# Norm of two attention heads: 16 normalising operations written on GpSimd instead of VectorE

## The chip, the core and the metric

The kernel runs on one core of a Trainium2 chip. Its time is the device time of one execution in microseconds (us); the time of a kernel is the median of several executions. The engines of the core are TensorE (PE in the profile, its weight loads PEld), VectorE (DVE), ScalarE (ACT), GpSimd (POOL) and SyncE (SP), which issues the transfers. Each engine works through its own list of instructions in the order in which they are written, and stops at an instruction until the semaphores that it names have reached their counts.

## The reference

Four layers, each an attention step and a feed-forward step, on x of 8 batches x 128 tokens x 128 features, float32. What the change touches is the layer norm ahead of the attention of layers 1 and 3 (the kernel's first and third softmax attention; layer 0's is another kind):

```python
def _layernorm(x, axis=-1, eps=1e-05):
    m = jnp.mean(x, axis=axis, keepdims=True)
    v = jnp.var(x, axis=axis, keepdims=True)
    return (x - m) / jnp.sqrt(v + eps)
...
    x = x + jnp.tanh(g_ffn[0]) * _L0_ffn_ref(_layernorm(x, axis=-1), ...
    x = x + jnp.tanh(g_xattn[1]) * _L1_xattn_ref(_layernorm(x, axis=-1), ctx_1024, ctx_1024, ...
    x = x + jnp.tanh(g_ffn[1]) * _L1_ffn_ref(_layernorm(x, axis=-1), ...
    x = x + jnp.tanh(g_xattn[2]) * _L2_xattn_ref(_layernorm(x, axis=-1), ctx_1024, ctx_1024, ...
    x = x + jnp.tanh(g_ffn[2]) * _L2_ffn_ref(_layernorm(x, axis=-1), ...
    x = x + jnp.tanh(g_xattn[3]) * _L3_xattn_ref(_layernorm(x, axis=-1), ctx_1024, ...
    x = x + jnp.tanh(g_ffn[3]) * _L3_ffn_ref(_layernorm(x, axis=-1), ...
```

Queries of an attention come from the normed x, keys and values from the context, which does not change. So keys and values can be projected while x is still being finished; queries cannot.

## The kernel before

Every tensor lies with the 128 tokens of a batch on the partitions; X and XN are 128 x 8 batches x 128. Work on all tokens is done in two halves of four batches. There is no scheduler: the functions below write each engine's list by hand, and an engine meets its work in that order.

A norm numbered k runs in these steps. VectorE writes the statistics of a half (`half_stats_dve`: four `bn_stats` into STAT, L394, and four `bn_aggr` into MV, L400). GpSimd makes 1/sqrt(v + eps) of a half in two instructions on 128x4 numbers (`norm_pool`: VE, L447, then the power RSTD, L449). Then each batch is normed, one instruction of 128x128 per batch (`ln_apply`, L410, into XN; each raises the semaphore `ln_xn` by one). TensorE transposes XN batch by batch into PSUM (`turn_pe`, L460), ScalarE copies the half to fp16 as XH (`turn_act`, L466), and VectorE writes the remainder XL (`turn_dve`, L472).

The head of attention a (`head_pe`, `head_act`, `head_dve`) runs 16 projections of keys and queries, numbered e = 0 to 15 (e 0 to 3 keys of the first half, 4 to 7 keys of the second, 8 to 11 and 12 to 15 queries), and two of values. One projection of keys or queries is three matmuls of 512 columns (L228), one ScalarE copy (`proj_act`, L1781, semaphore `p_hi`) and one VectorE operation of 128x512 (`proj_dve`, L1788, semaphore `p_lo`). TensorE may run at most four projections ahead of VectorE, by waits on `p_lo`. Projections 13 to 15 are woven into the first rows of the attention, whose maxima VectorE takes with L1914.

Heads a = 0 and a = 2 use norms k = 2 and k = 6. TensorE's order there: projections 2, 3, the values, the four transposes of the first half, projections 4 and 5, the four transposes of the second half, projections 6 to 12. The middle attention, a = 1, has a head of its own, which is not touched. `att_pool`, the GpSimd part of the attention, follows `norm_pool(pool, 2)` and `norm_pool(pool, 6)` in GpSimd's list. It already norms six of eight batches of the next norm itself, with the same `ln_apply`, in attention 0 and in attention 2.

Of the kernel before, what the change touches and what calls it, by code (L numbers as in the profile page):

```python
# [40 lines left out]
def gated_mix_program(nc, t, out):  # L41
# [5 lines left out]
    with ctx:  # L47
# [5 lines left out]
        def sem(name):  # L53
            if name not in sems:
                sems[name] = ctx.enter_context(nc.semaphore(name))
            return sems[name]
# [351 lines left out]
        def ln_apply(eng, k, b, s, to, src=X):  # L408
            eng.wait_ge(sem("ln_rstd"), NB * k + b + 1)
            eng.tensor_scalar(XN[:, to, :], src[:, b, :], MV[:, s, 0:1], RSTD[:, s:s + 1],  # L410
                              ALU.subtract, ALU.mult).then_inc(sem("ln_xn"), 1)
# [18 lines left out]
        def half_stats_dve(dve, k, i):  # L430

            for b in range(4 * i, 4 * i + 4):
                if k == 4:
                    dve.wait_ge(sem("x_quant"), b + 1)
                ln_stats(dve, k, b, b)
            for b in range(4 * i, 4 * i + 4):
                ln_mean(dve, k, b, b)

        def half_apply_dve(dve, k, i):
            for b in range(4 * i, 4 * i + 4):  # L440
                ln_apply(dve, k, b, b, b)

        def norm_pool(pool, k, halves=(0, 1)):
            for i in halves:
                h = slice(4 * i, 4 * i + 4)
                pool.wait_ge(sem("ln_mv"), NB * k + 4 * i + 4)
                pool.tensor_scalar(VE[:, h], MV[:, h, 1], 1e-5, None, ALU.add).then_inc(sem("ln_var"), 4)  # L447
                pool.wait_ge(sem("ln_var"), NB * k + 4 * i + 4)
                pool.tensor_tensor(RSTD[:, h], VE[:, h], EPS[:], ALU.pow).then_inc(sem("ln_rstd"), 4)  # L449


        def turn_pe(pe, j, k, halves=(0, 1), at=(0, 1)):
            if j == 0:
                pe.wait_ge(sem("ld_eye"), 16)
            for b in range(4 * halves[0], 4 * halves[-1] + 4):
                if j == 1 and b >= 4:
                    fill_pe(pe, 4, 2 if b == NB - 1 else 4)
                pe.wait_ge(sem("ln_xn"), NB * k + b + 1)
                to = tail_bank(7, 8) if j == 1 and b == 7 else bank(at[b // 4])[:, 128 * (b % 4):128 * (b % 4) + 128]
                pe.transpose(to, XN[:, b, :], EYE[:])\  # L460
                    .then_inc(sem("xt_turned"), 1)
# [7 lines left out]
        def turn_dve(dve, j, halves=(0, 1), at=(0, 1)):  # L469
            for i in halves:  # L470
                dve.wait_ge(sem("xt_high"), NB * j + 4 * (i + 1))
                dve.tensor_tensor(XL[:, 4 * i:4 * i + 4, :].rearrange("p b s -> p (b s)"), bank(at[i]),  # L472
                                  XH[:, 4 * i:4 * i + 4, :].rearrange("p b s -> p (b s)"),
                                  ALU.subtract).then_inc(sem("xt_low"), 4)
# [1217 lines left out]
        def moe_x_dve(dve, m, i):  # L1692

            g = 4 + (0, 2, 3)[m]
            dve.wait_ge(sem("y_turned"), 2 * m + i + 1)
            xs = X[:, 4 * i:4 * i + 4, :].rearrange("p b d -> p (b d)")
            dve.scalar_tensor_tensor(xs, bank(i), G[:, g:g + 1], xs, ALU.mult, ALU.add).then_inc(sem("x_moe"), 1)
            if m < 2:
                dve.wait_ge(sem("x_moe"), 2 * m + i + 1)
# [84 lines left out]
        def proj_dve(dve, a, e):  # L1784
            done, c, i, g = proj_place(a, "kq", e)
            dve.wait_ge(sem("p_hi"), 16 * a + e + 1)
            dst = (KU if c == "k" else QU)[:, g, 4 * i:4 * i + 4, :].rearrange("p b s -> p (b s)")
            dve.scalar_tensor_tensor(dst, proj_bank(a, "kq", e), BQK[:, a, "qk".index(c), g:g + 1], TLO[:, e % 4, :],  # L1788
                                     ALU.add, ALU.subtract).then_inc(sem("p_lo"), 1)
# [53 lines left out]
        def head_dve(dve, a):  # L1843

            k = NORM[a]
            if a != 1:
                for i in range(2):
                    moe_x_dve(dve, a // 2, i)
                    half_stats_dve(dve, k, i)
                half_apply_dve(dve, k, 0)  # L1850
                for e in (0, 1):
                    proj_dve(dve, a, e)
                half_apply_dve(dve, k, 1)
                turn_dve(dve, TURN[a], (0,), TURN_AT)
                for e in (2, 3, 4):
                    proj_dve(dve, a, e)
                turn_dve(dve, TURN[a], (1,), TURN_AT)
                for e in range(5, 13):
                    proj_dve(dve, a, e)
            else:  # L1860
                quant_front_dve(dve, 1)
                proj_dve(dve, a, 0)
                half_apply_dve(dve, k, 0)
                quant_round_dve(dve, 1)
                proj_dve(dve, a, 1)
                turn_dve(dve, TURN[a], (0,), TURN_AT)
                for e in (2, 3):
                    proj_dve(dve, a, e)
                quant_x_dve(dve, 1)
                half_stats_dve(dve, k, 1)  # L1870
                for e in range(4, 8):
                    proj_dve(dve, a, e)
                half_apply_dve(dve, k, 1)
                for e in (8, 9):
                    proj_dve(dve, a, e)
                turn_dve(dve, TURN[a], (1,), TURN_AT)
                for e in range(10, 13):
                    proj_dve(dve, a, e)
# [438 lines left out]
        def quant_front_dve(dve, i):  # L2317
            quant_max_dve(dve, i)
            quant_scale_dve(dve, i)

        def quant_round_dve(dve, i):

            h, at = HF4[i], 8 * i
            dve.wait_ge(sem("q_step"), at + 6)
            dve.tensor_scalar(XS[:, h, :], XS[:, h, :], ROUND, ROUND, ALU.add, ALU.subtract).then_inc(sem("q_step"), 1)
            if i == 0:
                dve.wait_ge(sem("ld_late"), 16 * len(LATE))
            dve.tensor_scalar(AMX[:, 1, h], AMX[:, 0, h], WSC[:, 0:1], G[:, 5:6], ALU.mult, ALU.mult)\
                .then_inc(sem("q_step"), 1)
            dve.wait_ge(sem("q_step"), at + 8)  # L2330
            dve.tensor_scalar(XQ[:, h, :], XS[:, h, :], 127.0, -128.0, ALU.min, ALU.max).then_inc(sem("q_rounded"), 1)
# [22 lines left out]
        def quant_bias_pool(pool, b):  # L2354

            if b == 0:
                pool.wait_ge(sem("fb1_gained"), 1)
            pool.wait_ge(sem("ln_xn"), 3 * NB + b + 1)
            pool.tensor_tensor(X[:, b, :], X[:, b, :], FB1G[:], ALU.add).then_inc(sem("x_biased"), 1)

        def quant_x_dve(dve, i):

            dve.wait_ge(sem("q_product"), i + 1)
            for b in range(4 * i, 4 * i + 4):
                dve.wait_ge(sem("x_biased"), b + 1)
                dve.scalar_tensor_tensor(X[:, b, :], bank(Q_PROD[i])[:, 128 * (b % 4):128 * (b % 4) + 128], AMX[:, 1, b:b + 1],
                                         X[:, b, :], ALU.mult, ALU.add).then_inc(sem("x_quant"), 1)
# [5 lines left out]
        @block.sync  # L2373
        def _(sp):
            sp_loads(sp)
            moe_loads(sp, 0)
            t5_sp(sp)
            moe_loads(sp, 1)
            moe_loads(sp, 2)
            for i in range(2):  # L2380
                h = slice(4 * i, 4 * i + 4)
                sp.wait_ge(sem("x_moe"), 5 + i)
                sp.dma_start(out[:, h, :], X[:, h, :]).then_inc(sem("stored"), 16)
            sp.wait_ge(sem("stored"), 32)

        @block.gpsimd
        def _(pool):
            pool_consts(pool)
            norm_pool(pool, 0)
            mlstm_pool(pool)  # L2390
            moe_pool(pool, 0)
            norm_pool(pool, 2)
            att_pool(pool, 0)
            norm_pool(pool, 4, (0,))
            for b in (NB - 2, NB - 1):
                quant_bias_pool(pool, b)
            norm_pool(pool, 4, (1,))
            pool.wait_ge(sem("ld_late"), 16 * len(LATE))
            att_pool(pool, 1)
            threefold(pool, 2)  # L2400
            moe_pool(pool, 1)
            norm_pool(pool, 6)
            att_pool(pool, 2)
            moe_pool(pool, 2)

# [168 lines left out]
```

## Time and profile before

| | us |
|---|---|
| median of 3 runs | 644.99 |
| lowest and highest | 644.38 and 647.12 |
| the profiled execution, its own time | 648.96 |
| the span of its instructions | 647.2 |
| busy in that span: TensorE, VectorE, ScalarE, GpSimd | 567.3, 518.1, 340.5, 249.4 |

The profile is of one execution. Its span runs from the first to the last instruction, and 1.76 us of its time lie around it. The stretches that matter here are the head of the first attention (about 129 to 146 us) and that of the third (about 512 to 530 us). Times of rows are counted from the start of the span. Back-to-back operations of an engine overlap a little, so the distance of two starts is somewhat less than one duration.

### The profile page before, as it was taken

How to read it: one execution, taken by the hardware profiler on the slowest of the kernel's cores; microseconds unless marked ns; L12 is line 12 of the kernel's file. 1: busy time of each engine (PE TensorE's matmuls, PEld its weight loads, DVE VectorE, ACT ScalarE, POOL GpSimd, SP SyncE). 2: the span in 40 equal slices, each digit the busy share in tenths (PEclk: the TensorE clock that was granted, in tenths of full speed). 3: DMA queues.
4: the chain of work that ended last, by engine and by line, in shares of the span. 5: the costliest groups of instructions: out<-in, count | busy, mean ns of one | idle time of the engine just before them, and what ended most of it. 6: DMA issues, size and time to landing. Idle time of an engine off the chain costs nothing.

```text
span 647.2 us, 16313 instructions
## 1 busy us (share of the span) xinstructions
PE 567.3 (88%) x5394; PEld 292.8 (45%) x5394; DVE 518.1 (80%) x1136; ACT 340.5 (53%) x675; POOL 249.4 (39%) x456
## 2 busy tenths in 40 slices
PE   4899888987977789967999999999999779996897
PEld 2444567834653345533444344343434325553443
DVE  6798845696889868856799999999999796766886
ACT  4778735664654533433455555555555454333554
POOL 3474000210584068773244444344443100234462
PEclk9999978996998999987899999999999899997999
DMA  8500200060000000001466665666666000001110
GB/s 324 196 2 2 68 3 3 2 151 2 4 2 1 2 1 3 2 3 36 134 180 172 168 172 171 166 177 178 177 169 170 27 2 2 2 3 30 31 53 34
DMA packets 34912, 48.89 MB, mean 76 GB/s; under 512 B 6756, under 2 KB 26800, under 8 KB 34472
## 3 DMA queue, kind: packets, MB, share of 16 engines
q1 hardware_dynamic: 34424, 47.40, 25.8%
q8 instruction: 37, 0.61, 0.4%
q10 hardware_dynamic: 432, 0.73, 0.3%
q14 instruction: 19, 0.16, 0.1%
HBM read 47.29 MB, written 0.82 MB: 74 GB/s over the span
## 4 chain that ended last, share of the span: by engine, by line
PE 43%; DVE 41%; ACT 7%; issue 4%; POOL 3%; DMA 1%; DVEq 0%; ACTq 0%; SPq 0%; POOLq 0%
PE PS L228 30%; DVE PS L1115 8%; DVE SHARED L1264 4%; DVE SHARED L1788 4%; PE PS L2020 2%; DVE PS L1128 2%; ACT SHARED L1093 2%; PE PS L2026 2%; ACT SHARED L1064 2%; PE PS L1892 2%; DVE MB L1914 2%; DVE PS L1914 2%; DVE STAT L394 2%; DVE REC L2034 1%; DVE XN L410 1%
## 5 line engine op out<-in xcount | busy, mean ns | idle before, releaser
L228 PE MATMUL PS<-XH,UH 128*128 128x512 f16 x232 | 91.0, 392 | 5.4 <-DVE PS L1115 3.3
L1093 ACT ACTIVATE SHARED<-PS 128x512 f16<-128x512 f32 x96 | 57.1, 597 | 72.5 <-DVE PS L1128 67.7
L228 PE MATMUL PS<-XL,UH 128*128 128x512 f16 x232 | 90.1, 389 | 0.0
L228 PE MATMUL PS<-XH,UL 128*128 128x512 f16 x232 | 90.0, 388 | 0.0
L2001 ACT ACTIVATE SHARED<-PS 128x512 f32<-128x512 f32 x96 | 52.1, 594 | 64.0 <-PE PS L228 48.8
L228 PE MATMUL PS<-SHARED,DNH 128*128 128x512 f16 x232 | 69.0, 379 | 4.6 <-DVE SHARED L1264 3.7
L1064 ACT ACTIVATE SHARED<-PS 128x512 f32<-128x512 f32 x96 | 57.2, 597 | 20.1 <-PE PS L228 15.1
L1264 DVE TENSOR_TENSOR SHARED<-PS,SHARED 128x512 f16<-128x512 f32 x96 | 62.0, 687 | 6.8 <-ACT SHARED L1093 3.4
L1022 POOL CAST DNH<-DF 128x128 f16<-128x128 f32 x58 | 19.6, 338 | 119.7 <-DMA DF<-in_down 95.0
L1128 DVE TENSOR_TENSOR PS<-PS,SHARED 128x512 f32<-128x512 f32 x92 | 59.7, 695 | 3.8
L1115 DVE TENSOR_TENSOR PS<-SHARED,PS 128x1024 f32<-128x1024 f32 x46 | 56.6, 1230 | 6.7 <-PE PS L228 0.7
L1914 DVE TENSOR_REDUCE MB<-PS 128x4 f16<-128x512 f32 x64 | 41.1, 688 | 17.0 <-PE PS L228 11.0
L2005 POOL TENSOR_TENSOR SHARED<-SHARED,GPT 128x512 f32<-128x512 f32 x32 | 40.0, 1273 | 24.3 <-ACT SHARED L2001 24.3
L1781 ACT ACTIVATE SHARED<-PS,LOB,LOM 128x512 f16<-128x512 f32 x48 | 35.4, 775 | 26.0 <-PE PS L228 26.0
L228 PEld LDWEIGHTS PS<-XH,UH 128*128 128x128 f16 x232 | 23.1, 99 | 50.8 <-DVE PS L1115 24.6
L228 PE MATMUL PS<-SHARED,DNL 128*128 128x512 f16 x116 | 44.1, 380 | 0.0
L1015 POOL TENSOR_TENSOR UL<-UF,UH 128x256 f16<-128x256 f32 x58 | 38.9, 671 | 4.6
L2020 PE MATMUL PS<-SHARED,ONE 128*32 128x128 f32 x768 | 40.5, 284 | 0.0
L2026 PE MATMUL PS<-SHARED,V 128*32 128x128 f32 x768 | 39.4, 277 | 0.6 <-POOL SHARED L2005 0.6
L1788 DVE SCALAR_TENSOR_TENSOR SHARED<-PS,BQK,SHARED 128x512 f16<-128x512 f32 x48 | 33.6, 740 | 6.0 <-ACT SHARED L1781 5.9
L228 PEld LDWEIGHTS PS<-SHARED,DNH 128*128 128x128 f16 x232 | 22.2, 98 | 33.6 <-issue 7.1
L228 PEld LDWEIGHTS PS<-XH,UL 128*128 128x128 f16 x232 | 23.2, 100 | 29.1 <-issue 3.0
(345 smaller groups left out, 1285.8 us busy)
## 6 DMA issues: line engine op xcount, KB each, us to landing
SHARED<-w_rows_dram SPq DMA_DIRECT2D x31, 384.0 KB, 3.7
SHARED<-w_rows_dram SPq DMA_DIRECT2D x30, 256.0 KB, 3.7
UF<-in_up SPq DMA_DIRECT2D x58, 128.0 KB, 3.4
SHARED<-w_rows_dram SPq DMA_DIRECT2D x31, 128.0 KB, 2.9
DF<-in_down SPq DMA_DIRECT2D x58, 64.0 KB, 2.9
V<-in_up SPq DMA_DIRECT2D x2, 1024.0 KB, 8.3
SHARED<-in_down SPq DMA_DIRECT2D x4, 512.0 KB
SHARED<-t_values_dram SPq DMA_DIRECT2D x2, 1024.0 KB, 10.4
```

The source lines that it names most:

```text
L228: last = pe.matmul(dst, l, r, start=start and i == 0, stop=stop and i == len(pairs) - 1)
L1064: act.activation(SG1[u][:, hf, :], bank(hf), ACT.Silu).then_inc(sem("e_act"), 1)
L1093: act.activation(HHI[:, u, hf, :], bank(4 + hf) if m == 1 else HF[:, hf, :], ACT.Copy).then_inc(sem("e_high"), 1)
L1115: dve.tensor_tensor(dst, SG1[u].rearrange("p i n -> p (i n)"), bank(2, 2), ALU.mult).then_inc(sem("w1_gated"), 1)
L1128: dve.tensor_tensor(bank(4 + hf), bank(4 + hf), WB[u][:, HALF * hf:HALF * hf + HALF], ALU.mult)\
L1264: dve.tensor_tensor(HLO[:, u, hf, :], src, HHI[:, u, hf, :], ALU.subtract).then_inc(sem("e_low"), 1)
L1788: dve.scalar_tensor_tensor(dst, proj_bank(a, "kq", e), BQK[:, a, "qk".index(c), g:g + 1], TLO[:, e % 4, :], ALU.add, ALU.subtract).then_in ...
L1914: dve.tensor_reduce(dst, src, AX, ALU.max, negate=True).then_inc(sem("a_max"), 1)
L2001: act.activation(PF[:, j, :], bank(2 + j % 2), ACT.Exp).then_inc(sem("a_exp"), 1)
L2005: pool.tensor_tensor(PG[:, j, :].rearrange("p (g s) -> p g s", g=4), PF[:, j, :].rearrange("p (g s) -> p g s", g=4), over(GPT[:, b, :], 4) ...
L2020: pe.matmul(bank(4 + u)[32 * g:32 * g + 32, 128:256], ONE8[:, j, :], PF[:, j, 128 * g:128 * g + 128], start=j == 0, stop=j == 3, skip_grou ...
L2026: last = pe.matmul(bank(4 + u)[32 * g:32 * g + 32, 0:128], V32[:, b, 4 * g + j, :], src[:, j, 128 * g:128 * g + 128], start=False, stop=j ...
```

## The change

`norm_pool(pool, 2)` and `norm_pool(pool, 6)` become `head_pool(pool, 2)` and `head_pool(pool, 6)`. That function writes, for each half, the same two instructions for RSTD and then the four normings of that half, on GpSimd. `head_dve` loses its two calls of `half_apply_dve` for a = 0 and a = 2. Nothing else is written differently; `norm_pool` takes the half as an argument already.

```diff
+        def head_pool(pool, k):
+            for i in range(2):
+                norm_pool(pool, k, (i,))
+                for b in range(4 * i, 4 * i + 4):
+                    ln_apply(pool, k, b, b, b)
...
                 for i in range(2):
                     moe_x_dve(dve, a // 2, i)
                     half_stats_dve(dve, k, i)
-                half_apply_dve(dve, k, 0)
                 for e in (0, 1):
                     proj_dve(dve, a, e)
-                half_apply_dve(dve, k, 1)
                 turn_dve(dve, TURN[a], (0,), TURN_AT)
...
-            norm_pool(pool, 2)
+            head_pool(pool, 2)
             att_pool(pool, 0)
...
-            norm_pool(pool, 6)
+            head_pool(pool, 6)
             att_pool(pool, 2)
```

GpSimd's list at the head of the first attention, before. L1728 at the top prepares the weights of this attention, at the bottom those of the next.

```order
L1728 COPY WRL<-WL 128x32x24
L447 TENSOR_SCALAR VE<-MV 128x4
L449 TENSOR_TENSOR RSTD<-VE,EPS 128x4
L447 TENSOR_SCALAR VE<-MV 128x4
L449 TENSOR_TENSOR RSTD<-VE,EPS 128x4
L1728 COPY WRH<-WH 128x32x24
```

The same place after (line numbers below L449 are 7 or 5 higher there):

```order
L1735 COPY WRL<-WL 128x32x24
L447 TENSOR_SCALAR VE<-MV 128x4
L449 TENSOR_TENSOR RSTD<-VE,EPS 128x4
L410 TENSOR_SCALAR XN<-X,MV,RSTD 128x128 x4
L447 TENSOR_SCALAR VE<-MV 128x4
L449 TENSOR_TENSOR RSTD<-VE,EPS 128x4
L410 TENSOR_SCALAR XN<-X,MV,RSTD 128x128 x4
L1735 COPY WRH<-WH 128x32x24
```

Four normings now stand between the first power and the second VE, and four behind the second power.

VectorE's list at the head of the third attention, before. L1697 adds the feed-forward result to X; of L1788 each is one projection.

```order
L1697 SCALAR_TENSOR_TENSOR X<-PS,G,X 128x512
L394 BN_STATS STAT<-X 128x6 x4
L400 BN_AGGR MV<-STAT 128x2 x4
L410 TENSOR_SCALAR XN<-X,MV,RSTD 128x128 x4
L1788 SCALAR_TENSOR_TENSOR SHARED<-PS,BQK,SHARED 128x512 x2
L410 TENSOR_SCALAR XN<-X,MV,RSTD 128x128 x4
L472 TENSOR_TENSOR XL<-PS,XH 128x512
L1788 SCALAR_TENSOR_TENSOR SHARED<-PS,BQK,SHARED 128x512 x3
L472 TENSOR_TENSOR XL<-PS,XH 128x512
L1788 SCALAR_TENSOR_TENSOR SHARED<-PS,BQK,SHARED 128x512 x8
```

The same place after:

```order
L1704 SCALAR_TENSOR_TENSOR X<-PS,G,X 128x512
L394 BN_STATS STAT<-X 128x6 x4
L400 BN_AGGR MV<-STAT 128x2 x4
L1795 SCALAR_TENSOR_TENSOR SHARED<-PS,BQK,SHARED 128x512 x2
L479 TENSOR_TENSOR XL<-PS,XH 128x512
L1795 SCALAR_TENSOR_TENSOR SHARED<-PS,BQK,SHARED 128x512 x3
L479 TENSOR_TENSOR XL<-PS,XH 128x512
L1795 SCALAR_TENSOR_TENSOR SHARED<-PS,BQK,SHARED 128x512 x8
```

The eight normings are gone from it, and what stood around them keeps its order. TensorE's and ScalarE's lists do not change.

## Rows read from the trace of the kernel before

**Rows 1.** Chain that ended last, first and third head: start us, length us, engine, tile, line.

```profile
132.85 1.03 DVE XN L410 x4
...
516.41 1.03 DVE XN L410 x4
517.44 1.14 DVE SHARED L1788 x2
...
518.68 1.10 DVE XN L410 x4
519.78 0.60 DVE XL L472
```

**Rows 2.** VectorE in order of time, third head: start us, duration us, instruction.

```profile
522.28 0.67 DVE L472 TENSOR_TENSOR XL<-PS,XH 128x512 f16<-128x512 f32 x1
522.88 5.34 DVE L1788 SCALAR_TENSOR_TENSOR SHARED<-PS,BQK,SHARED 128x512 f16<-128x512 f32 x8
```

**Rows 3.** VectorE in order of time, first head; in brackets idle time before it.

```profile
138.71 0.68 DVE L472 TENSOR_TENSOR XL<-PS,XH 128x512 f16<-128x512 f32 x1
139.31 4.69 DVE L1788 SCALAR_TENSOR_TENSOR SHARED<-PS,BQK,SHARED 128x512 f16<-128x512 f32 x7
145.07 0.75 DVE L1788 SCALAR_TENSOR_TENSOR SHARED<-PS,BQK,SHARED 128x512 f16<-128x512 f32 x1 [1.07 <-ACT SHARED L1781]
```

**Rows 4.** GpSimd in order of time, first head.

```profile
131.57 1.05 POOL L449 TENSOR_TENSOR RSTD<-VE,EPS 128x4 f32<-128x4 f32 x1
133.01 0.37 POOL L447 TENSOR_SCALAR VE<-MV 128x4 f32<-128x4 f32 x1 [0.39 <-DVE MV L400]
133.52 1.11 POOL L449 TENSOR_TENSOR RSTD<-VE,EPS 128x4 f32<-128x4 f32 x1
151.09 0.82 POOL L1728 COPY WRH<-WH 128x768 f16<-128x768 f16 x1 [16.46 <-PE PS L228]
```

**Rows 5.** GpSimd in order of time, third head.

```profile
514.76 0.23 POOL L447 TENSOR_SCALAR VE<-MV 128x4 f32<-128x4 f32 x1 [11.16 <-DVE MV L400]
515.14 1.05 POOL L449 TENSOR_TENSOR RSTD<-VE,EPS 128x4 f32<-128x4 f32 x1
```

**Rows 6.** All normings by L410: duration ns least/median/most, first and last start.

```profile
L410 DVE TENSOR_SCALAR XN<-X,MV,RSTD x38: 314/340/397, 7.5 to 592.5; 128x128 f32<-128x128 f32 x38
L410 POOL TENSOR_SCALAR XN<-X,MV,RSTD x12: 809/811/815, 168.8 to 586.8; 128x128 f32<-128x128 f32 x12
```

**Rows 7.** GpSimd in order of time, within the third attention.

```profile
553.49 0.58 POOL L406 TENSOR_TENSOR RSTD<-VE,EPS 128x1 f32<-128x1 f32 x1
554.18 0.81 POOL L410 TENSOR_SCALAR XN<-X,MV,RSTD 128x128 f32<-128x128 f32 x1
554.95 0.43 POOL L2053 TENSOR_TENSOR ATL<-AT,ATH 128x128 f16<-128x128 f32 x1
```

**Rows 8.** ScalarE in order of time, third head: the copies that make XH.

```profile
517.92 0.60 ACT L466 ACTIVATE XH<-PS 128x512 f16<-128x512 f32 x1 [1.59 <-PE PS L460]
...
520.36 0.59 ACT L466 ACTIVATE XH<-PS 128x512 f16<-128x512 f32 x1
```

**Rows 9.** TensorE in order of time, end of the stage before and third head.

```profile
509.09 0.63 PE L228 MATMUL PS<-CHI,WRH 128*128 128x512 f16 x1
...
510.37 0.63 PE L228 MATMUL PS<-CHI,WRH 128*128 128x512 f16 x1
...
516.70 1.12 PE L460 MATMUL PS<-EYE,XN 128*128 128x128 f32 x4 [1.01 <-DVE XN L410]
```

**Rows 10.** Stretches: us, busy of PE, PEld, DVE, ACT, POOL, granted clock, DMA share, GB/s.

```profile
504.00:508.00 4.00, 1.41 (x8) 0.46 (x7) 3.77 (x6) 1.20 (x2) 0.00 (x0) 1.00 0.06 16
508.00:510.00 2.00, 2.00 (x9) 0.79 (x8) 0.20 (x1) 1.19 (x2) 0.00 (x0) 0.75 0.00 0
510.00:512.00 2.00, 2.00 (x7) 0.98 (x6) 0.00 (x0) 0.88 (x2) 0.00 (x0) 0.50 0.00 0
512.00:514.00 2.00, 2.00 (x14) 1.40 (x13) 1.31 (x4) 0.93 (x2) 0.00 (x0) 0.90 0.00 0
```

## The prediction

> **What bounds the kernel now.** I read the chain of work that ended last first, because only what lies on it can move the time. In both heads it runs through VectorE almost without a break: the eight normings of each head are links of it, followed by the projections of L1788 and the remainders XL [rows 1]. So VectorE is the bound of the heads, and taking work off it looks right. Next I read the engines in order of time, for what else is late. GpSimd makes the two powers and then stands idle for 16.46 us behind the first head [rows 4]. It has room; whether it is quick enough is the question, since the normings are links of a chain and not loose work. What to watch is the start of the second XL, at 138.71 us in the first head and at 522.28 in the third [rows 2, 3]. Behind it VectorE works through seven or eight projections in a row at 0.66 us each, and the attention starts at the end of that row. Whatever the second XL loses or gains, the start of the attention loses or gains.
>
> **What the change removes.** Four normings of 1.03 us and four of 1.10 us leave VectorE's list in the third head [rows 1], 2.1 us per head, 4.3 us in all. Would the second XL then wait for VectorE alone, it would start 2.1 us earlier. That is the largest gain that a head can give.
>
> **What it adds, and where.** The same instruction runs twelve times on GpSimd in this kernel, in 809 to 815 ns, against 340 ns on VectorE [rows 6]. Its distance to the next GpSimd instruction is 0.77 us (554.18 to 554.95), and it starts 0.11 us behind the end of its power (553.49 + 0.58 = 554.07, then 554.18) [rows 7]. On VectorE four stand 1.03 us apart, 0.26 each [rows 1]. The price is thus three times as high, not twice, and that from a row of the same instruction, so there is nothing to bound from afar. All the same a wait per instruction could stand between two of them, which no row shows for a run of four; as an upper end I take 0.81 + 0.11 = 0.92 us for the distance.
>
> The second consequence is one of order. GpSimd makes the second half's power only behind the first half's four normings. Before, that power was done beside VectorE's first normings and cost nothing. Now its 0.38 us from VE to power (514.76 to 515.14) and its 1.05 us [rows 5] are on the path.
>
> **The sum for one head**, from the end P of the first power to the second XL:
> first four normings 0.11 + 4 x 0.77 = 3.19;
> VE and power of the second half 0.38 + 1.05 = 1.43;
> last four normings 0.11 + 3 x 0.77 + 0.81 = 3.23;
> the relay over TensorE and ScalarE. Before, the last norming ended at 519.78 [rows 1] and the ScalarE copy started at 520.36 and took 0.59 [rows 8], 1.19 with 0.02 for the semaphore; for the first half it is 517.44, 517.92 and 0.60 [rows 1, 8], 1.10. I take 1.15.
> Together 9.00 us behind P.
>
> First head: P = 131.57 + 1.05 = 132.62 [rows 4], XL at 141.62 in place of 138.71, 2.91 us later. Third head: P = 515.14 + 1.05 = 516.19 [rows 5], XL at 525.19 in place of 522.28, again 2.91 us later. The earlier XL, of the first half, is late too (P + 0.11 + 3.12 + 1.15, 520.57 in the third head in place of 519.78), but between it and the second one VectorE has only three projections, 2.0 us, and is done with them by about 523.2. It then waits for GpSimd. The 2.1 us that it was relieved of turn into idle time ahead of the two XL.
>
> **What lies behind.** The second XL is followed by projections 5 to 11 or 12. TensorE gets to projection 6 when the last transpose is out, about 0.5 us behind the last norming, and ScalarE makes XH first. Projection 5 is ready, and from 6 on both engines need 0.65 and 0.67 us for each, VectorE 0.66; they keep just ahead, as before. So the whole delay is passed on: no edge of slack is visible between [rows 2, 3]. GpSimd itself is free again at about 140.5 and 524.0 us, long before its next work at 151.09 [rows 4] plus the delay; nobody waits for that. The change issues no DMA and moves none.
>
> One thing is read off rows that look alike. With VectorE norming beside it, GpSimd took 0.37 us for VE and 1.11 for the power [rows 4]; without, 0.23 and 1.05 [rows 5]. The first pair no longer happens, so I used the second. The Trainium skill (SBUF — State Buffer, Who interferes with whom) says that GpSimd and VectorE share one pair of ports, which is locked for a whole instruction, and that a VectorE instruction with at most one SBUF input outside a two-port mode leaves it alone. By that rule these two rows are a collision, and the projections and XL that now run beside the normings, which read PSUM and one SBUF tensor, cause none; the sum stays.
>
> **TensorE's clock.** Between 504 and 508 us TensorE was busy 1.41 us of 4, and from 509 to 512 the granted clock was at the lower of the two levels (1.2 in place of 2.4 GHz) [rows 10]. Three matmuls then took 1.28 us (509.09 to 510.37) [rows 9] in place of 0.65. After the change TensorE has between 515.7 and 519.7 us nothing but four transposes, each 0.8 us behind the other, about 0.3 us of work each; before, it waited 1.01 us and did all four in 1.12 [rows 9]. That stretch is as empty as the one at 504 us, so the clock will probably fall in the third head. It would slow projections 4 and 5, which VectorE does not wait for, and the last transposes by 0.2 us. I add 0.2 us.
>
> **The number.** 2 x 2.91 + 0.2 = 6.0 us. Against the profiled execution that is 648.96 + 6.0 = 655.0 us, or 653.2 us of span. That execution stands 3.97 us above the median of the runs, which I take to be the profiling; against the median it is 644.99 + 6.0 = 651.0 us, 0.9% slower.
>
> **Rivals.**
> First, the clock costs more. If it falls late, while the second half's transposes trickle in (137.6 to 140.8 us in the first head, 521 to 524.4 in the third), the projections from 6 on run at 1.28 us apiece and VectorE's row starves. The low stretch of [rows 10] lasted some 3.5 us (all of 510 to 512, half of 508 to 510 and a fifth of 512 to 514, by the means there, make 3.4), so a head loses up to 1.7 us more. One head: 652.7; both: 654.4. For it: four transposes in 3.3 us. Against it: two projections just ahead of them. Chance 0.17.
> Second, it gets faster. Place: the second XL. VectorE alone would reach it 2.1 us earlier, in both heads 4.2 us, 640.8 us. It decides at the GpSimd distance p for which P + 2.84 + 8p is no later than before: with 6.09 us from 516.19 to 522.28, p = 0.41 us. GpSimd does 128x128 in 0.43 us where it subtracts into fp16 [rows 7], which speaks for it; the twelve rows of the same instruction at 0.81 [rows 6] speak against it. Chance 0.02.
> Third, GpSimd costs less than its rows, but not that little. With p = 0.51, twice VectorE's 0.26, a head loses 2.84 + 4.08 - 6.09 = 0.8 us, 646.6 us in all. The Trainium skill (GPSIMD Engine Reference, 3.1 Elementwise — side-by-side cycle accounting) measures GpSimd at 1.96 times VectorE for a large add; here a small instruction with two per-partition numbers is at three times, by this case's trace. Chance 0.03.
> Fourth, one head's delay is absorbed in the attention behind it. VectorE has a wait of 1.07 us ahead of projection 12 in the first head [rows 3]. But that wait follows its own projection 10 and moves with it. 644.99 + 3.1 = 648.1 us. Chance 0.05.
> That the change doesn't do what it says is excluded by the two lists shown.
>
> **How the numbers follow.** The forecast has 0.73. With the upper distance of 0.92 us a head costs 7 x 0.15 = 1.1 us more, 653.1 us, which lies within the range as the clock's one and two heads do, at 652.7 and 654.4. Downwards it has to reach the absorbed head at 648.1 to leave out no more than the two cheap cases; 648.2 to 654.8. A measurement of this kernel can tell about 0.5% from no change, 641.8 to 648.2 us. Faster: the second rival, 0.02. Within: the third, and the fourth, 0.08. Slower: forecast and clock, 0.90.
>
> **What would show it.** In the profile after: GpSimd's L410 sixteen times more, at 0.81 us and 0.77 apart; the second XL of each head about 9.0 us behind the end of the first power; idle time of VectorE ahead of both XL, about 2.8 and 2.0 us in the third head, ended by ScalarE; and GpSimd on the chain with about 6 us per head, where it was not. The span would be 5.8 to 6.2 us longer, half of it at each head, with nothing changed in between. It would be wrong if the run of four is quicker than single ones, if VectorE's projections behind the second XL have gaps (the clock), or if the attention starts less late than its second XL.

## The result

The changed kernel is slower, by about what was forecast.

| | before | after |
|---|---|---|
| median, us | 644.68 (6 runs) | 650.38 (6 runs) |
| lowest and highest | 643.18 and 647.12 | 649.02 and 652.48 |
| ratio, 95% interval | | 1.0095, 1.0067 to 1.0123 |
| span of the profiled execution | 647.2 | 649.7 |

The forecast was 651.0 us, in a range from 648.2 to 654.8. The ratio makes 6.1 us (4.3 to 7.9), the forecast 6.0. The interval is much wider than the 0.1 us between these two, so a match as close as this is in part luck; what tests the forecast is the second XL of each head in the profile.

To compare heads across executions I measure each from the start of the addition that finishes the first half of X (L1697 before, L1704 after, called the zero of the head) to the start of the first row maximum of the attention. GpSimd in order of time, first head after; the columns are start, duration, instruction and, in brackets, idle time:

```profile
129.92 0.23 POOL L447 TENSOR_SCALAR VE<-MV 128x4 f32<-128x4 f32 x1 [5.69 <-DVE MV L400]
130.30 1.05 POOL L449 TENSOR_TENSOR RSTD<-VE,EPS 128x4 f32<-128x4 f32 x1
131.45 3.15 POOL L410 TENSOR_SCALAR XN<-X,MV,RSTD 128x128 f32<-128x128 f32 x4
134.57 0.24 POOL L447 TENSOR_SCALAR VE<-MV 128x4 f32<-128x4 f32 x1
134.96 1.04 POOL L449 TENSOR_TENSOR RSTD<-VE,EPS 128x4 f32<-128x4 f32 x1
136.10 3.13 POOL L410 TENSOR_SCALAR XN<-X,MV,RSTD 128x128 f32<-128x128 f32 x4
```

Where [rows 4] had two powers 1.95 us apart, they are now 4.66 apart, with 3.15 us of norming between them and 3.13 behind. VectorE in the same head:

```profile
127.82 0.75 DVE L1704 SCALAR_TENSOR_TENSOR X<-PS,G,X 128x512 f32<-128x512 f32 x1 [1.58 <-PE PS L228]
...
131.49 1.38 DVE L1795 SCALAR_TENSOR_TENSOR SHARED<-PS,BQK,SHARED 128x512 f16<-128x512 f32 x2
135.93 0.69 DVE L479 TENSOR_TENSOR XL<-PS,XH 128x512 f16<-128x512 f32 x1 [3.06 <-ACT XH L473]
136.53 2.06 DVE L1795 SCALAR_TENSOR_TENSOR SHARED<-PS,BQK,SHARED 128x512 f16<-128x512 f32 x3
140.40 0.69 DVE L479 TENSOR_TENSOR XL<-PS,XH 128x512 f16<-128x512 f32 x1 [1.81 <-ACT XH L473]
141.01 4.69 DVE L1795 SCALAR_TENSOR_TENSOR SHARED<-PS,BQK,SHARED 128x512 f16<-128x512 f32 x7
146.77 0.75 DVE L1795 SCALAR_TENSOR_TENSOR SHARED<-PS,BQK,SHARED 128x512 f16<-128x512 f32 x1 [1.07 <-ACT SHARED L1788]
147.44 1.28 DVE L1919 TENSOR_REDUCE MB<-PS 128x4 f16<-128x512 f32 x2
```

The four normings are gone twice, and VectorE waits 3.06 and 1.81 us instead, both times for ScalarE's XH, which waits for TensorE's transposes, which wait for GpSimd. The second XL stands 12.58 us behind the zero, against 9.62 before (138.71 less 129.09, [rows 3]). From there on the rows are those of before: seven projections in 4.69 us, a wait of 1.07 us, one more.

The chain that ended last, third head after (start, length, engine, tile, line). VectorE's normings [rows 1] have made room for GpSimd:

```profile
514.29 1.06 POOL RSTD L449
...
515.44 0.17 POOL XN L410
515.61 0.63 issue
516.24 2.34 POOL XN L410 x3
518.58 0.22 POOL VE L447
...
518.94 1.03 POOL RSTD L449
...
520.08 3.14 POOL XN L410 x4
...
523.26 0.33 PE PS L467
523.59 3.62 PE PS L228 x9
```

The last line was not expected there: behind the last transpose the chain runs through nine matmuls in 3.62 us. TensorE in order of time and the granted clock in stretches (busy of PE, PEld, DVE, ACT, POOL, then the clock) show why:

```profile
523.42 0.38 PE L228 MATMUL PS<-CHI,WRH 128*128 128x512 f16 x1
523.64 0.57 PE L228 MATMUL PS<-CLO,WRH 128*128 128x512 f16 x1
524.00 0.63 PE L228 MATMUL PS<-CHI,WRL 128*128 128x512 f16 x1
524.43 0.63 PE L228 MATMUL PS<-CHI,WRH 128*128 128x512 f16 x1
```

```profile
520.00:522.00 2.00, 0.85 (x4) 0.28 (x2) 2.00 (x4) 1.10 (x2) 1.93 (x3) 1.00 0.00 0
522.00:524.00 2.00, 1.11 (x5) 0.49 (x5) 0.43 (x1) 0.32 (x1) 1.20 (x2) 0.92 0.03 8
524.00:526.00 2.00, 2.00 (x6) 0.76 (x5) 1.62 (x3) 1.10 (x3) 0.00 (x0) 0.50 0.02 4
526.00:528.00 2.00, 2.00 (x8) 0.83 (x7) 1.14 (x2) 1.50 (x3) 0.00 (x0) 0.72 0.00 0
```

TensorE had been busy 1.96 us of the 4 from 520 to 524, two thirds of it in four thin transposes. The clock went to its lower level (1.2 GHz) within projection 6, at about 523.8 us, and was low through projections 7 and 8, until about 527.1. VectorE's row of projections then has gaps that [rows 2] does not have:

```profile
519.76 0.69 DVE L479 TENSOR_TENSOR XL<-PS,XH 128x512 f16<-128x512 f32 x1 [2.91 <-ACT XH L473]
...
524.38 0.69 DVE L479 TENSOR_TENSOR XL<-PS,XH 128x512 f16<-128x512 f32 x1 [1.96 <-ACT XH L473]
524.99 1.40 DVE L1795 SCALAR_TENSOR_TENSOR SHARED<-PS,BQK,SHARED 128x512 f16<-128x512 f32 x2
526.76 0.75 DVE L1795 SCALAR_TENSOR_TENSOR SHARED<-PS,BQK,SHARED 128x512 f16<-128x512 f32 x1 [0.37 <-ACT SHARED L1788]
528.04 3.42 DVE L1795 SCALAR_TENSOR_TENSOR SHARED<-PS,BQK,SHARED 128x512 f16<-128x512 f32 x5 [0.53 <-ACT SHARED L1788]
531.81 1.29 DVE L1919 TENSOR_REDUCE MB<-PS 128x4 f16<-128x512 f32 x2 [0.34 <-PE PS L228]
```

The heads are 19.62 and 20.01 us long, before 16.64 and 15.92: 2.98 and 4.09 us more, 7.1 in all. Yet the profiled span grew by only 2.5 us. The rest of the kernel has the same instructions and was 4.6 us shorter in this execution than in the profiled one before: the first head's zero came 1.27 us earlier (127.82, before 129.09), between the first head's end and the third's zero lie 364.36 us in place of 366.93, and behind the third head 117.89 in place of 118.62. That is a warning for reading two profiles: the difference of two spans mixes the change with what any two executions differ by. Heads measured from their own zero are much steadier: where the clock stays at its upper level, the same head comes out alike to 0.02 us in the profiles below.

### The profile page after: what moved, and what is told of

Its sections match the earlier page's. It is cut to its first block, busy times and chain, and to the rows that moved or that the text cites. A ratio compares the mean times of both kernels' runs of the same rounds, so it can differ in the third digit from the quotient of the medians.

```text
span 649.7 us, 16313 instructions
## 1 busy us (share of the span) xinstructions
PE 567.8 (87%) x5394; PEld 292.4 (45%) x5394; DVE 513.7 (79%) x1120; ACT 340.7 (52%) x675; POOL 260.7 (40%) x472
## 4 chain that ended last, share of the span: by engine, by line
PE 44%; DVE 37%; ACT 7%; POOL 6%; issue 4%; DMA 1%; DVEq 0%; ACTq 0%; POOLq 0%; SPq 0%
PE PS L228 31%; DVE PS L1122 8%; DVE SHARED L1271 4%; DVE SHARED L1795 3%; PE PS L2025 2%; DVE PS L1135 2%; POOL XN L410 2%; ACT SHARED L1100 2%; PE PS L2031 2%; ACT SHARED L1071 2%; DVE MB L1919 2%; PE PS L1897 2%; DVE PS L1919 2%; DVE REC L2039 1%; DVE STAT L394 1%
## 5 line engine op out<-in xcount | busy, mean ns | idle before, releaser
L1788 ACT ACTIVATE SHARED<-PS,LOB,LOM 128x512 f16<-128x512 f32 x48 | 35.4, 774 | 23.4 <-PE PS L228 23.3
```

## The experiments

All numbers of heads are from the one profile of the named kernel; ratios are against the kernel before, run on the same chip beside it. The table stands ahead, the readings behind. "XL2" is the start of the second XL behind the zero of the head.

| kernel | XL2, first and third head | length of the heads | both heads against before | ratio and interval |
|---|---|---|---|---|
| before | 9.62, 9.62 | 16.64, 15.92 | | 1 |
| changed kernel | 12.58, 12.58 | 19.62, 20.01 | +7.07 | 1.0095, 1.0067 to 1.0123 |
| first head only | 12.75, 9.63 | 20.41, 15.92 | +3.77 | 1.0069, 1.0036 to 1.0103 |
| third head only | 9.62, 12.61 | 16.64, 18.92 | +3.00 | 1.0039, 1.0012 to 1.0067 |
| second half only | 10.03, 10.04 | 17.07, 16.35 | +0.86 | 1.0013, 0.9983 to 1.0042 |
| powers first | 13.23, 13.22 | 20.27, 19.54 | +7.25 | 1.0089, 1.0055 to 1.0122 |
| fill matmuls | 13.11, 12.59 | 20.15, 18.90 | +6.49 | 1.0096, 1.0070 to 1.0121 |
| half width | 10.85, 10.84 | 17.88, 17.15 | +2.47 | 1.0027, 0.9990 to 1.0064 |
| normings doubled | 18.99, 18.98 | 28.20, 26.84 | +22.5 | 1.0340, 1.0281 to 1.0400 |
| ScalarE, both heads | 9.67, 9.04 | 16.70, 15.34 | -0.52 | 0.9976, 0.9953 to 1.0000 |
| ScalarE, third head | 9.63, 9.04 | 16.65, 15.34 | -0.57 | 0.9994, 0.9970 to 1.0017 |
| ScalarE, both, again | 9.67, 9.18 | 16.70, 15.66 | -0.20 | 0.9985, 0.9963 to 1.0007 |

**One head at a time.** In the first kernel the third head is undone, in the second the first:

```diff
+                if a == 2:
+                    half_apply_dve(dve, k, 0)
                 for e in (0, 1):
                     proj_dve(dve, a, e)
+                if a == 2:
+                    half_apply_dve(dve, k, 1)
...
-            head_pool(pool, 6)
+            norm_pool(pool, 6)
```

> The change in the first head alone; the third head has its eight normings on VectorE again, as before. I measure a head from the start of the first VectorE operation that adds the feed-forward result to X (L1697 before) to the start of the first row maximum (L1914 before): before 16.64 us in the first head and 15.92 in the third, after the change 19.62 and 20.01. Theory (each head pays on its own because its normings are links of the chain): first head 19.6 us, third head 15.9, the whole kernel 3.0 us slower than before, ratio 1.0046. Rival (one head's delay is absorbed behind it and the other carries all): the whole is either 0 or 6 us slower, ratio 1.000 or 1.009.

> The change in the third head alone; the first head as before. Theory: first head 16.6 us, third head 18.9 if TensorE's clock stays at its upper level behind the transposes and 20.0 if it falls as in the profile of the changed kernel; the whole 3.0 to 4.1 us slower than before, ratio 1.005 to 1.006. Rival (absorbed): ratio 1.000 or 1.009, the opposite of what the first head alone gives.

Each head pays for itself. Absorption wanted 1.000 for one of the two kernels and 1.009 for the other; they are 4.4 and 2.5 us slower than before, both intervals leave out 1.000, and that of the third head alone leaves out 1.009 too. The untouched head has its old length to 0.01 us. With the first head alone that head came out at 20.41 us instead of 19.6, of which 0.17 is a later XL2 and 0.62 follows it: in that execution the clock fell during projection 4 and was still low behind the transposes:

```profile
140.73 0.47 PE L467 MATMUL PS<-EYE,XN 128*128 128x128 f32 x1 [0.30 <-POOL XN L410]
141.00 0.63 PE L228 MATMUL PS<-CHI,WRH 128*128 128x512 f16 x1
...
143.13 0.52 PE L228 MATMUL PS<-CHI,WRL 128*128 128x512 f16 x1
143.49 0.38 PE L228 MATMUL PS<-XH,WRH 128*128 128x512 f16 x1
```

With the third head alone that head took 18.92 us, with the same instructions that took 20.01 in the changed kernel. Its stretches:

```profile
512.00:516.00 4.00, 2.23 (x6) 0.96 (x7) 1.09 (x2) 0.54 (x1) 3.85 (x6) 0.77 0.00 0
516.00:520.00 4.00, 3.06 (x11) 1.31 (x10) 2.67 (x4) 1.66 (x4) 3.37 (x5) 0.80 0.02 4
520.00:524.00 4.00, 3.74 (x18) 1.23 (x16) 3.35 (x6) 3.74 (x6) 0.00 (x0) 1.00 0.01 2
```

Here the clock fell earlier, at the third transpose of the first half (514.1 us), and was back at 517.7. Four transposes and projections 4 and 5 were slowed, ahead of the last normings; the clock was full when projection 6 came at 519.7. So the same thinly used stretch costs 0 or 1.1 us in the third head, by where in it the clock falls.

**Second half only.** VectorE norms the first half, GpSimd the second behind both powers:

```diff
-            for i in range(2):
-                norm_pool(pool, k, (i,))
-                for b in range(4 * i, 4 * i + 4):
-                    ln_apply(pool, k, b, b, b)
+            norm_pool(pool, k)
+            pool.wait_ge(sem("ln_xn"), NB * k + 4)
+            for b in range(4, NB):
+                ln_apply(pool, k, b, b, b)
```

> In both heads GpSimd norms only the second half, behind both powers; VectorE norms the first half as before. Theory (the cost is GpSimd's time in series, not the handing over to another engine): the second power ends about 5.4 us behind the first addition to X, then 0.11 + 3.12 for four normings and 1.15 for the relay, second XL 9.8 to 9.9 us behind it, against 9.62 before and 12.58 after the change. Heads 16.9 and 16.2 us, the whole 0.2 to 0.7 us slower than before, ratio 1.0005 to 1.001, nothing that can be told from no change. Rival (handing the normings over costs by itself, by waits and by TensorE's idle time): half of the full loss, 3 us, ratio 1.0045.

XL2 is 10.03 us, 0.1 to 0.2 later than expected, and the interval of the ratio just leaves out the rival's 1.0045. Handing four normings per head to GpSimd costs 0.4 us, handing it eight 3 us: it is GpSimd's time in series that counts, not that another engine does it. VectorE was relieved of four normings here too, and that brought nothing.

**Powers first.**

```diff
-            for i in range(2):
-                norm_pool(pool, k, (i,))
-                for b in range(4 * i, 4 * i + 4):
-                    ln_apply(pool, k, b, b, b)
+            norm_pool(pool, k)
+            for b in range(NB):
+                ln_apply(pool, k, b, b, b)
```

> As the changed kernel, but GpSimd makes both powers first and then all eight normings. My prediction put the second half's VE and power, 1.43 us, on the path by their place behind four normings. If that place is what costs (theory A), taking them from there gains 1.4 us per head: second XL 11.15 us behind the first addition to X, against 12.58 after the change; the whole 3.2 us slower than before, ratio 1.005. If it is GpSimd's total work that costs (theory B), nothing is gained: the second power can't end sooner than 5.3 us behind that addition, because its statistics are ready only at 3.75; 0.11 + 7 x 0.77 + 0.81 + 1.15 more make 12.7 to 12.9 us for the second XL; the whole 6 to 6.5 us slower, ratio 1.0095 to 1.010.

Theory A falls: the kernel is no faster than the changed one. GpSimd in the third head (zero at 513.40):

```profile
515.88 1.05 POOL L449 TENSOR_TENSOR RSTD<-VE,EPS 128x4 f32<-128x4 f32 x1
517.32 0.23 POOL L447 TENSOR_SCALAR VE<-MV 128x4 f32<-128x4 f32 x1 [0.39 <-DVE MV L400]
517.70 1.03 POOL L449 TENSOR_TENSOR RSTD<-VE,EPS 128x4 f32<-128x4 f32 x1
518.73 6.26 POOL L410 TENSOR_SCALAR XN<-X,MV,RSTD 128x128 f32<-128x128 f32 x8
```

GpSimd waits for nobody behind 517.32 and ends at 524.99, 11.59 us behind the zero, where the changed kernel ended at 11.41 (520.08 + 3.13 less 511.80). With the changed kernel's 1.17 us of relay that would put XL2 at 12.76, within theory B's 12.7 to 12.9. It came at 13.22, 0.46 us later: projections 4 and 5 now stand right ahead of the second half's transposes, ran at the lower clock until 524.76, and the four transposes queued behind them.

**Half width.** The norming in both heads on 64 of the 128 features:

```diff
-                    ln_apply(pool, k, b, b, b)
+                    pool.wait_ge(sem("ln_rstd"), NB * k + b + 1)
+                    pool.tensor_scalar(XN[:, b, 0:64], X[:, b, 0:64], MV[:, b, 0:1], RSTD[:, b:b + 1],
+                                       ALU.subtract, ALU.mult).then_inc(sem("ln_xn"), 1)
```

> The changed kernel with the normings on GpSimd in both heads done on 64 of the 128 features only; the other half of XN keeps what stood there, so the queries of the two attentions are not those of the reference. It makes GpSimd's distance p smaller and nothing else. My formula for the second XL behind the first addition to X is 3.53 + 2.84 + 8p = 6.37 + 8p, which the 0.78 us of the changed kernel fit with 12.6. Between 0.23 us (four columns) and 0.81 (128), half the width should give 0.52 us a piece and p of 0.47 to 0.50: second XL at 10.1 to 10.4 us, heads 17.2 and 16.5, the whole 1.0 to 1.5 us slower than before, ratio 1.002. With p at 0.41 it would be even. Rival (the price is fixed per instruction or per hand-over): p stays near 0.78 and nothing is gained.

```profile
515.27 2.28 POOL L458 TENSOR_SCALAR XN<-X,MV,RSTD 128x64 f32<-128x64 f32 x4
517.51 0.24 POOL L447 TENSOR_SCALAR VE<-MV 128x4 f32<-128x4 f32 x1
```

Four take 2.24 us from start to the next instruction, p = 0.56, not the 0.47 to 0.50 that I had worked out. Half the columns do not make half the time: from 0.78 and 0.56 a line through both has 0.34 us at no columns. With the measured p the formula gives 6.37 + 8 x 0.56 = 10.85, and 10.84 to 10.85 is what the two heads show. The formula holds, my estimate of p did not. By the same line the p of 0.41, at which the change would be even, is reached at some 20 columns.

**Normings doubled.**

```diff
                 for b in range(4 * i, 4 * i + 4):
+                    pool.wait_ge(sem("ln_rstd"), NB * k + b + 1)
+                    pool.tensor_scalar(CF[:, b, :], X[:, b, :], MV[:, b, 0:1], RSTD[:, b:b + 1],
+                                       ALU.subtract, ALU.mult)
                     ln_apply(pool, k, b, b, b)
```

> The changed kernel with each of the 16 normings on GpSimd done twice, the first time into a buffer that nobody reads. Theory (every GpSimd distance of 0.78 us stands on the path, eight per head): second XL 6.2 us later than in the changed kernel, 18.8 us behind the first addition to X, in both heads; heads 25.9 and 25.2 to 26.3 us, the whole 18.4 to 19.5 us slower than before, ratio 1.028 to 1.030. Rival (part of the normings is covered, by the projections or by the next head's work): clearly less than 6.2 us per head.

XL2 is 6.4 us later than in the changed kernel, 0.80 per added norming: nothing is covered. The heads are longer than expected by more, 2.3 us in the first and at least 0.5 in the third. The stretches show the clock again; TensorE has 1.3 us of work in four while GpSimd norms, and runs at the lower level for most of the head, through the projections behind XL2 as well:

```profile
528.00:532.00 4.00, 1.19 (x3) 0.57 (x4) 0.00 (x0) 0.00 (x0) 3.92 (x6) 0.50 0.00 0
532.00:536.00 4.00, 3.25 (x8) 0.94 (x6) 2.67 (x4) 2.15 (x3) 3.83 (x5) 0.50 0.02 4
536.00:540.00 4.00, 1.44 (x4) 0.73 (x5) 0.00 (x0) 0.00 (x0) 3.46 (x5) 0.50 0.00 0
540.00:544.00 4.00, 4.00 (x11) 1.38 (x10) 2.69 (x4) 2.29 (x4) 0.00 (x0) 0.51 0.01 2
```

**Fill matmuls.**

```diff
+                if j in (2, 5) and b >= 4:
+                    fill_pe(pe, 1, 2)
                 pe.wait_ge(sem("ln_xn"), NB * k + b + 1)
```

> The changed kernel with two idle matmuls of 512 columns written ahead of each of the four transposes of the second half in both heads (into a PSUM bank that nobody reads), so that TensorE does not stand idle between them. In the profile of the changed kernel the granted clock fell to 0.50 from 524 to 526 us, behind those transposes in the third head, and the head took 20.01 us in place of the 18.9 that its second XL gave reason for. Theory (the extra 1.1 us is TensorE's clock): no low clock behind the second half's transposes, third head 18.9 to 19.1 us, first head 19.6 to 19.8; the whole 1 us faster than the changed kernel at most, ratio to before 1.008 to 1.009. Rival (the extra 1.1 us is something else, or the matmuls delay the transposes by as much as they save): third head 20 us or more.

Third head 18.90 us with no low clock, as expected; but the third head alone gave 18.92 without fill, so this run doesn't prove that the fill did it. The first head missed what was expected, with 20.15 us: the clock had fallen at 132 us already, ahead of the fill, the first idle matmuls then ran at half speed ahead of the transposes, and XL2 came at 13.11, 0.53 us later than in the changed kernel. The ratio is that of the changed kernel. Whether a fill helps on the mean is left open.

**ScalarE for the second half.** VectorE norms the first half in both heads; GpSimd works out -mean x rstd of four batches, ScalarE norms them between its first XH and projection 4, and makes the second XH ahead of projection 5:

```diff
             turn_act(act, TURN[a], (0,), TURN_AT)
...
-                for e in (4, 5):
-                    proj_act(act, a, "k", e)
+                act.wait_ge(sem("ln_xn"), NB * NORM[a] + 4)
+                for b in range(4, NB):
+                    act.wait_ge(sem("ln_nmr"), (6 if a == 0 else 18) + b - 3)
+                    act.activation(XN[:, b, :], X[:, b, :], ACT.Identity, bias=NMR[:, b:b + 1], scale=RSTD[:, b:b + 1])\
+                        .then_inc(sem("ln_xn"), 1)
+                proj_act(act, a, "k", 4)
             turn_act(act, TURN[a], (1,), TURN_AT)
```

> In both heads VectorE norms the first half as before, and ScalarE norms the second, with a factor and an addend (GpSimd works out the addend, four small instructions behind both powers); ScalarE does that between its first XH and projection 4, and makes the second XH behind projection 4. Theory (what counts is when the second XL can start; ScalarE norms in 0.42 us where GpSimd takes 0.78, and the power is ready 5.5 us behind the first addition to X): ScalarE norms from 5.9 to 7.6 us, projection 4 to 8.3, XH to 9.0, second XL at 9.1 in place of 9.62 before; heads 16.1 and 15.4 us, the whole 1.0 us faster than before, ratio 0.998 to 0.999, which can be told from before by the heads only. Rival (ScalarE is needed by the projections there): second XL at 9.6 or later, ratio 1.000 or more.

> ScalarE norms the second half in the third head only; the first head is as before, in order and engines. In the run with both heads changed the first head gave 16.70 us against 16.64 before (nothing) and the third 15.34 against 15.92. Theory (only the third head gains, since in the first ScalarE comes late from the values): first head 16.6, third 15.3, the whole 0.6 us faster than before, ratio 0.999, not to be told from before by the whole time. Rival (the run with both heads was faster in the whole by 1.5 us for a reason outside the heads): ratio 0.997 or 0.998 here too.

> The kernel in which ScalarE norms the second half in both heads, once more, for a narrower interval: before it was 0.9976 with an interval from 0.9953 to 1.0000, while its heads give only 0.5 us, ratio 0.9992. Theory (the heads are all that changed): ratio 0.998 to 1.000, with 0.9992 within the interval. Rival (there is a gain outside the heads): 0.9976 again, with an interval that leaves out 0.9992.

ScalarE's normings in the first head, then ScalarE in the third:

```profile
132.93 1.64 ACT L1849 ACTIVATE XN<-X,NMR,RSTD 128x128 f32<-128x128 f32 x4
...
512.88 0.60 ACT L475 ACTIVATE XH<-PS 128x512 f16<-128x512 f32 x1 [1.60 <-PE PS L469]
513.64 1.65 ACT L1849 ACTIVATE XN<-X,NMR,RSTD 128x128 f32<-128x128 f32 x4 [0.16 <-POOL NMR L458]
515.19 0.76 ACT L1790 ACTIVATE SHARED<-PS,LOB,LOM 128x512 f16<-128x512 f32 x1
515.86 0.58 ACT L475 ACTIVATE XH<-PS 128x512 f16<-128x512 f32 x1
```

Four normings in 1.65 us; GpSimd takes 3.14. In the third head XL2 comes 0.58 us earlier than before (0.44 in the repeat, where the clock was partly low there). In the first it gains nothing, against what was expected: ScalarE is held up by the second values and starts norming 6.67 us behind the zero (132.93 less 126.26) where the third head has 6.03 (513.64 less 507.61). The edit also puts the second XH ahead of projection 5. That alone can't be the gain: before, this copy ended at 520.95 [rows 8], 1.3 us ahead of the second XL at 522.28, which did not wait for it. Two measurements of the kernel with both heads gave 0.9976 and 0.9985. Both lie below 1, and both intervals hold the 0.9992 that the heads account for; one holds 1 and the other ends there. The third head alone gave 0.9994, which holds 0.9992 and also the rival's 0.998, so a small gain outside the heads is not excluded. The kernel beats the changed one clearly; that it beats the kernel before in the whole is likely and not shown, in the third head it is shown.

## Why the prediction was right

**The term that carries the sum** was right to 0.05 us: the second XL 9.00 us behind the end of the first power; it was 9.05 in the first head (131.35 to 140.40) and 9.04 in the third (515.34 to 524.38). All its parts are there: distance 0.78 for 0.77, VE and power undisturbed at 0.24 and 1.04 where [rows 4] had 0.37 and 1.11, the relay 1.17 for 1.15. It came out because the price was read from the very instruction on the very engine [rows 6, 7]. That VectorE's projections and XL do not slow the normings came out too: four take 3.15 us beside the first two projections and 3.13 beside XL and the next three, and in the kernel with the normings doubled they stand 0.78 us apart from 528 to 532 us, where VectorE does nothing.

**That VectorE's relief is worth nothing** was right. It waits 2.91 and 1.96 us ahead of the two XL of the third head, where 2.8 and 2.0 were named, and the kernel with the second half alone shows it once more.

**Why the second power counts** was put wrongly. The prediction gave 1.43 us of the loss to its place behind four normings. Made first, it saved nothing. VE and power are on the path because GpSimd is busy without a gap from the second statistics on; in whichever order, its 6.3 us of norming and the powers stand behind each other. The sum was right, since it added GpSimd's work in series, but the reason beside the term was not.

**TensorE's clock** was the weak term. I added 0.2 us for a fall in the third head that would slow projections 4 and 5 at no cost and the last transposes by 0.2 us. In the profile of the changed kernel it fell behind them and cost 1.1 us, which is the first rival in one head; in the first head it fell early (low from 134.7 to about 138 us) and cost nothing; with the third head alone it cost nothing there, with the first head alone 0.8 us in all there. The ground for the term was weak too: it rested on the stretch from 504 to 508 us, with 1.41 us of work and a low clock behind it [rows 10]; the changed kernel had 1.46 us of work in the same stretch and the full clock from 508 to 512. The term is 0 to 1.1 us a head by execution, and with normings doubled 1.6 to 2.2 behind XL2. What it is on the mean stays open: two heads without it are 6.0 us (2.98 in the changed kernel's first head, 3.00 with the third head alone), and the ratio says 6.1, with 7.9 at its upper end.

**The other rivals.** Nothing was absorbed: each head alone is slower. GpSimd at twice VectorE's price would have given a ratio of 1.0025 and is excluded by the interval, and by the distance of 0.78 us in the profile. The gain below p = 0.41 lies on the formula that half width confirmed at one more point, and a p that low was not run.

**What the prediction said of the spans** was wrong: 5.8 to 6.2 us more, with nothing changed in between, where the profiled spans differ by 2.5. The stages outside the heads moved by 4.6 us although their instructions are the same. TensorE's clock differed in them: added up over stretches of 2 us, the profiled execution before ran some 53 us outside the heads at the lower level, the changed one some 41. One place is [rows 10], right ahead of the third head, where VectorE waited 4.46 us for TensorE before the zero and 2.77 in the changed kernel; another is the first attention, low from 148 to 150 us before and not after. That all of the 4.6 us are the clock is likely and not shown. The prediction also took it that profiling makes an execution 3.97 us longer. The other kernels don't bear that out as a rule: the profiled execution lies anywhere from 1.2 us below (fill matmuls) to 4.0 above (first head alone) the median of its kernel. The profiled execution before was a long one: of 23 other executions of that kernel in one set, the 12 with a mean granted clock of 0.960 or less took 645.6 to 649.9 us, the 11 with more 642.1 to 644.9, and the profiled one had 0.959 and 648.96. In the two other sets the division is less clean.

## What to carry to other kernels

Work that is a link of a chain can't be given to an idle engine for nothing: multiply the idle engine's own distance for that instruction by the number in series, put the powers or copies that now queue with it beside it, and see whether the waiting engine's next step comes later. Four links of the eight fitted into the slack between power and second XL here but for 0.4 us; eight did not. ScalarE, with half the distance of GpSimd, did the same four at a gain of 0.6 us in the third head and at none in the first, where it came to them later. And measure a stage from its own first instruction, since the spans of two executions can differ by nearly as much as such a change.

## What the runs showed of the hardware

GpSimd's norming of 128x64 float32 stands 0.56 us from the next, that of 128x128 0.78: halving the columns saves 0.22 us of 0.78. ScalarE norms 128x128 at 0.39 us from start to start (513.64 to 515.19 for four), VectorE at 0.26.

In the heads GpSimd's two operations on 128x4 numbers took 0.37 us and 1.10 to 1.12 beside VectorE's normings (before, second half only, ScalarE in both heads) and 0.23 to 0.24 and 1.03 to 1.05 otherwise.

Thin work can go with a fall of TensorE's clock. Around transposes 0.78 us apart with 0.33 us of work each, the granted clock went from 1.0 to 0.5 in the changed kernel (134.7 and 523.8 us), with the first head alone (136.5) and with the third head alone (514.1). It stayed low for some 3.3 to 3.6 us in three of these cases, 6.9 us with the first head alone, and some 17 us where the thin work went on (normings doubled, third head). Where the clock falls changes from one execution to the next, and with it whether the fall costs anything.
